# Two-layer decoder on one core: row-sum reciprocals spread over DRAM, the attention result copied by ScalarE and scaled in place by Pool

## The reference, cut to what matters

```python
x = _layernorm(x + _L0_attn_ref(...));  x = _layernorm(x + _L0_ffn_ref(...))
# _L1_attn_ref:
latent_kv = x @ w_kv_down
k, v = split(latent_kv @ w_kv_up);  q = x @ w_q           # 16 heads of 64
att = jnp.einsum('bqhd,bkhd->bhqk', q, k) * HEAD_SIZE ** -0.5
att = jax.nn.softmax(jnp.where(causal, att, -jnp.inf), axis=-1)
y = jnp.einsum('bhqk,bkhd->bqhd', att, v)
x = _layernorm(x + y.reshape(Bx, Tx, HD) @ w_out);  x = _layernorm(x + _L1_ffn_ref(...))
```

## Time and profile before

| | us |
|---|---|
| median of 3 runs (range) | 1919.13 (1919.01 to 1919.22) |
| the profiled execution | 1919.19 |
| its span, first to last instruction | 1917.1 |

### The profile page before, as it was taken

One profiled execution on the slowest core, in us unless ns is written; L12 is line 12 of the kernel. 1 busy time (PEld: TensorE's weight loads), 2 busy tenths in 40 slices (PEclk: granted clock), 3 DMA queues, 4 the chain that ended last, 5 costly groups with the idle time before them and its releaser, 6 DMA issues. The chain is left out here.

```text
span 1917.1 us, 42317 instructions
## 1 busy us (share of the span) xinstructions
PE 1703.5 (89%) x15702; PEld 1445.2 (75%) x15702; DVE 1362.2 (71%) x3230; ACT 1000.8 (52%) x2618; POOL 619.1 (32%) x975
## 2 busy tenths in 40 slices
PE   4599999899999999999988598999999999998895
PEld 3477778787877778877876365688888888888794
DVE  4688777877788777877775475566666666664777
ACT  2355555555555555565543354556566656652353
POOL 6455345543555335543451122000000000001653
PEclk9799999999999999999988799999999999999898
DMA  6212331323222332323320200990000000003232
GB/s 216 59 51 65 75 86 49 68 59 85 65 56 65 75 87 46 74 67 75 83 50 23 90 1 5 183 14 2 2 2 2 1 2 1 2 2 107 65 93 76
DMA packets 150338, 106.78 MB, mean 56 GB/s; under 512 B 34132, under 2 KB 138648, under 8 KB 149240
## 3 DMA queue, kind: packets, MB, share of 16 engines
q1 hardware_dynamic: 147640, 98.95, 23.7%
q0 software_dynamic: 2496, 5.13, 0.8%
HBM read 86.06 MB, written 17.99 MB: 54 GB/s over the span
## 5 line engine op out<-in xcount | busy, mean ns | idle before, releaser
L593 POOL TENSOR_TENSOR kfull<-kt,pair_rows 128x512 f32<-128x512 f32 x128 | 143.6, 1122 | 517.2 <-ACT kt L381 513.5
L361 PE MATMUL ps<-xT,taps 128*128 128x128 f32 x2048 | 276.8, 278 | 0.1
L853 ACT COPY wt<-ps 32x128 f32<-32x128 f32 x512 | 131.7, 257 | 263.9 <-PE ps L748 256.9
L361 PEld LDWEIGHTS ps<-xT,taps 128*128 128x128 f32 x2048 | 258.7, 196 | 7.6 <-issue 7.2
L1687 DVE TENSOR_REDUCE b_nmax<-ps 128x1 f32<-128x128 f32 (+7 forms) x256 | 180.6, 752 | 72.9 <-PE ps L1524 72.9
L896 DVE TENSOR_TENSOR prod<-ps,mt 128x128 f32<-128x128 f32 x512 | 147.4, 288 | 78.6 <-PE ps L759 62.7
L748 PE MATMUL ps<-ident,w 128*128 128x128 f32 x512 | 162.9, 318 | 34.6 <-ACT wt L853 18.5
L1664 POOL COPY b_spread<-b_inv 128x256 f32<-128x256 f32 x64 | 25.8, 402 | 513.2 <-DVE b_inv L1690 513.2
L899 DVE TENSOR_REDUCE w<-prod 128x32 f32<-128x128 f32 x512 | 146.5, 286 | 17.5
L748 PEld LDWEIGHTS ps<-ident,w 128*128 128x128 f32 x512 | 88.1, 172 | 84.9 <-DVE w L899 73.6
L1616 ACT ACTIVATE b_prob_long<-ps,b_nmax 128x1024 f32<-128x1024 f32 (+3 forms) x128 | 121.4, 953 | 55.7 <-DVE b_nmax L1687 55.7
(11 more groups left out here) (308 smaller groups left out, 3843.2 us busy)
## 6 DMA issues: line engine op xcount, KB each, us to landing
decay<-ends_dram SPq DMA_DIRECT2D x256, 128.0 KB, 5.5
gn<-near_dram SPq DMA_DIRECT2D x32, 384.0 KB, 6.9
slots_dram<-zero SPq DMA_DIRECT2D x1, 9216.0 KB, 59.3
rr<-rates_dram SPq DMA_DIRECT2D x32, 256.0 KB, 4.5
sq<-rstd_dram SPq DMA_DIRECT2D x16, 512.0 KB, 3.6
wtap<-in_taps SPq DMA_DIRECT2D x4, 1024.0 KB, 11.2
f_w<-in_f_w SPq DMA_DIRECT2D x2, 2048.0 KB, 10.4
s_xb<-slots_dram SPq DMA_DIRECT2D x46, 64.5 KB, 1.8
```

Of the source, the lines that this page charges most:

```text
L361: mm = pe.matmul(part, lhsT=taps[:, tap, t * P:(t + 1) * P], rhs=xT[:, :, columns(at_next) - LOOK + tap:columns(at_next) - LOOK + tap + TS ...
L593: nc.gpsimd.tensor_tensor(kfull[:, n % 4, :, :], kt[:, n % 2, :].unsqueeze(1).to_broadcast([P, G, P]), cst["pair_rows"][:, :].unsqueeze(2) ...
L853: nc.scalar.copy(wt[rows, b, :], ps[rows, 2, 0:P]).then_inc(wt_kept[b], 1)
```

## The change

The two transposes of the reciprocals, the Pool copy `spread` and DVE's `divide` are gone. In their place:

- SP stores `inv` of unit w (128 x 4, elements of 4 bytes) to a DRAM scratch `recips_dram`, waits for the store, and loads it back twice, each time into 64 partitions, as `recipT` (two buffers). Before the store of unit w it waits for `y_done` of unit w-2.
- ACT copies the undivided result from bank 7 to its place in `yT` (`keep_values`), where it copied the reciprocals before. `values(w)` now waits for this copy (`o_kept`).
- Pool multiplies that place in `yT` by `recipT`, in place.
- From unit 2 on, DVE's `reciprocal` also waits until the store of unit w-2 has landed, since it overwrites `inv`.
- The two DMAs into `slots_dram` are issued by ACT, after its copies of the first projections and ahead of the exponential of unit 0. SP waits for them at the end of the stage, as before.

```diff
-        spread = sb("spread", [P, 2, 4, AD])
-        recipT = sb("recipT", [P, 2 * P])
+        recipT = sb("recipT", [P, 2, 2 * P])
+        recips_dram = nc.dram_tensor("recips_dram", (2, 4, P), F32).ap()
...
                     if w:
-                        pe.wait_ge(y_done, w)
+                        pe.wait_ge(o_kept, w)
...
-                def turn_recips(w):
-                    pe.wait_ge(spread_done, w + 1)
-                    for long in range(2):
-                        mm = pe.transpose(ps[:, 7, (2 + long) * P:(3 + long) * P],
-                                          spread[:, w % 2, 2 * long:2 * long + 2, :].rearrange("p h c -> p (h c)"),
-                                          cst["ident"][:, :])
                     mm.then_inc(o_done, 1)
...
-                def keep_recips(w):
+                def keep_values(w):
                     act.wait_ge(o_done, w + 1)
-                    nc.scalar.copy(recipT[:, :], ps[:, 7, 2 * P:4 * P]).then_inc(recip_kept, 1)
+                    nc.scalar.copy(y_of(w), ps[:, 7, 0:2 * P].rearrange("p (i n t) -> p i n t", i=2,
+                                                                        n=P // TS)).then_inc(o_kept, 1)
...
+                slots = blank[2].rearrange("(k p) e -> p k e", p=P)
+                act.wait_ge(fill_made, 2)
+                nc.scalar.dma_start(slots[:, :, 0:C], blank[1][:, :].unsqueeze(1).to_broadcast(
+                    [P, slots.shape[1], C])).then_inc(filled, 16)
+                nc.scalar.dma_start(slots[:, :, C:ROW], blank[0][:, :].bitcast(F32).unsqueeze(2),
+                                    allow_slow_non_contiguous=True).then_inc(filled, 16)
                 for w in range(W):
                     for j in range(4):
                         exponent(w, j)
...
             @block.sync
+                for w in range(W):
+                    slot = recips_dram[w % 2]
+                    if w >= 2:
+                        sp.wait_ge(y_done, w - 1)
+                    sp.wait_ge(recip_done, w + 1)
+                    sp.dma_start(slot.rearrange("j q -> q j"), inv[:, w % 2, :],
+                                 allow_slow_non_contiguous=True).then_inc(recip_stored, 16)
+                    sp.wait_ge(recip_stored, 16 * (w + 1))
+                    for h in range(2):
+                        sp.dma_start(recipT[AD * h:AD * h + AD, w % 2, :].rearrange("c (l q) -> c l q", l=2),
+                                     slot[h:4:2, :].partition_broadcast(AD)).then_inc(recip_in[w % 2], 16)
...
             @block.gpsimd
-                    pool.wait_ge(recip_done, w + 1)
-                    nc.gpsimd.tensor_copy(spread[:, w % 2, :, :], inv[:, w % 2, :].unsqueeze(2).to_broadcast(
-                        [P, 4, AD])).then_inc(spread_done, 1)
+                    pool.wait_ge(recip_in[w % 2], 32 * (w // 2 + 1))
+                    pool.wait_ge(o_kept, w + 1)
+                    nc.gpsimd.tensor_tensor(y_of(w), y_of(w), recipT[:, w % 2, :].rearrange(
+                        "p (i n t) -> p i n t", i=2, n=P // TS), ALU.mult).then_inc(y_done, 1)
...
             @block.vector
                     dve.wait_ge(exp_done, 4 * w + 4)
+                    if w >= 2:
+                        dve.wait_ge(recip_stored, 16 * (w - 1))
                     nc.vector.reciprocal(inv[:, w % 2, :], total[:, w % 2, :]).then_inc(recip_done, 1)
-                    if w:
-                        divide(w - 1)
```

More of the change, by code:

```diff
@@ L1412, in softmax_attention, with y_of @@
             "lat_done", "lat_kept", "piece_done", "piece_kept_a", "piece_kept_v"))
-        s_done, max_done, exp_done, recip_done, spread_done, t_done, t_kept_a, t_kept_v, o_done, recip_kept, y_done = (
-            sem(n) for n in ("s_done", "max_done", "exp_done", "recip_done", "spread_done", "t_done", "t_kept_a",
-                             "t_kept_v", "o_done", "recip_kept", "y_done"))
+        s_done, max_done, exp_done, recip_done, recip_stored, t_done, t_kept_a, t_kept_v, o_done, o_kept, y_done = (
+            sem(n) for n in ("s_done", "max_done", "exp_done", "recip_done", "recip_stored", "t_done", "t_kept_a",
+                             "t_kept_v", "o_done", "o_kept", "y_done"))
+        recip_in = [sem("recip_in0"), sem("recip_in1")]
         every = [fill_made, filled, lat_done, lat_kept, piece_done, piece_kept_a, piece_kept_v, s_done, max_done, exp_done, recip_done,
-                 spread_done, t_done, t_kept_a, t_kept_v, o_done, recip_kept, y_done]
+                 recip_stored, t_done, t_kept_a, t_kept_v, o_done, o_kept, y_done] + recip_in
         units = [(hp, b, k) for hp in range(NP) for b in range(B) for k in range(TT // 2)]
         W, PW = len(units), B * TT // 2
+        def y_of(w):
+            hp, b, k = units[w]
+            return y_row[:, hp, b, k:TT - k:TT - 1 - 2 * k, :, :]
         def tile_of(w, long):
@@ L1555, in values @@
                                 cols = slice(AD * h, AD * h + AD)
-                                pe.matmul(ps[cols, 7, long * P:(long + 1) * P], lhsT=v[:, f, b * TT + j, cols],
-                                          rhs=probT[:, at_probT(w, long, h * n + j), :], start=(j == 0), stop=(j == n - 1),
-                                          skip_group_check=True)
-                def turn_recips(w):
-                    pe.wait_ge(spread_done, w + 1)
-                    for long in range(2):
-                        mm = pe.transpose(ps[:, 7, (2 + long) * P:(3 + long) * P],
-                                          spread[:, w % 2, 2 * long:2 * long + 2, :].rearrange("p h c -> p (h c)"),
-                                          cst["ident"][:, :])
+                                mm = pe.matmul(ps[cols, 7, long * P:(long + 1) * P], lhsT=v[:, f, b * TT + j, cols],
+                                          rhs=probT[:, at_probT(w, long, h * n + j), :], start=(j == 0),
+                                               stop=(j == n - 1), skip_group_check=True)
                     mm.then_inc(o_done, 1)
@@ L1590, in _ @@
                         values(w - 1)
-                        turn_recips(w - 1)
                     pieces = slot_pieces(w)
@@ L1600, in _ @@
                 values(W - 1)
-                turn_recips(W - 1)
             @block.scalar
@@ L1633, in _ @@
                     if w:
-                        keep_recips(w - 1)
+                        keep_values(w - 1)
                     hp = w // PW
@@ L1644, in _ @@
                                 "p (j t) -> p j t", t=P)).then_inc(t_kept_a, 1)
-                keep_recips(W - 1)
+                keep_values(W - 1)
             @block.sync
             def _(sp):
-                slots = blank[2].rearrange("(k p) e -> p k e", p=P)
-                sp.wait_ge(fill_made, 2)
-                sp.dma_start(slots[:, :, 0:C], blank[1][:, :].unsqueeze(1).to_broadcast(
-                    [P, slots.shape[1], C])).then_inc(filled, 16)
-                sp.dma_start(slots[:, :, C:ROW], blank[0][:, :].bitcast(F32).unsqueeze(2),
-                             allow_slow_non_contiguous=True).then_inc(filled, 16)
+                for w in range(W):
[9 more added lines that the diff above has]
+                                     slot[h:4:2, :].partition_broadcast(AD)).then_inc(recip_in[w % 2], 16)
+                for slot in range(2):
+                    sp.wait_ge(recip_in[slot], 32 * (W // 2))
                 sp.wait_ge(filled, 32)
@@ L1671, in keep_v @@
                         piece_kept_v, 1)
-                def divide(w):
-                    hp, b, k = units[w]
-                    dve.wait_ge(recip_kept, w + 1)
-                    view = "p (i n t) -> p i n t"
-                    nc.vector.tensor_tensor(y_row[:, hp, b, k:TT - k:TT - 1 - 2 * k, :, :],
-                                            ps[:, 7, 0:2 * P].rearrange(view, i=2, n=2),
-                                            recipT[:, :].rearrange(view, i=2, n=2), ALU.mult).then_inc(y_done, 1)
                 for n, piece in list(enumerate(FIRST))[8:]:
@@ L1702, in _ @@
                         keep_v(hp + 1, ps[:, 6, :], ROUND[n][1])
-                divide(W - 1)
         stage_end(nc, every)
```

## The result

| | us |
|---|---|
| before, median of 4 runs (range) | 1919.18 (1919.01 to 1921.45) |
| after, median of 4 runs (range) | 2209.25 (2205.91 to 2212.49) |
| ratio after / before, 95% interval | 1.151 (1.149 to 1.153) |
| profiled execution of after, its span | 2212.49, 2210.7 |

What follows compares the result with a forecast made beforehand. The prediction took PE to set the pace, DVE and ACT having room. Its terms 45.7 + 2.4 - 17.3 + 3.3 - 2.1 + 0.5 made +32.5 us on 1919.1: 1951.6 us, range 1938 to 1969.

Steps and rivals of the forecast that it cites:

- Part 1: Start of the stage: two DMAs issued by ACT ahead of its exponentials hold it and delay unit 0, +45.7 us.
- the two readings: The 50.80 us issue: spent on the second DMA's own 18432 pieces, or waiting for room behind the first DMA's 9216 KB.
- The first rival: ACT is not held by issuing the two DMAs, parts 1 and 2 vanish: 1903.5 us, chance 0.12.
- Part 2: PE after idling for ACT: its first products run at the lower granted clock, +2.4 us.
- Part 3: PE does two transposes less in each of 64 units, 0.27 us each by distance of starts: -17.3 us.
- Part 4: Without DVE's division, PE's masks behind k=1 units wait less for DVE's chunk copies: 16 x 0.13 = -2.1 us.
- What is given back: Part of PE's gain lost in 16 k=0 units (+2.7) and the last 8 units (+0.6): +3.3 us.
- Part 5: Reciprocals' round trip over SP and Pool: about 6 us per unit of 8, nothing in the steady loop, +0.5 at stage end.
- The rival of 0.02: The round trip over DRAM takes over 16 us, two units, and lengthens each unit: far above 1970, chance 0.02.
- The tail of +0.5: End of the stage: the last reciprocal's store, loads and product finish at about 1741.0 against 1740.54, +0.5 us.
- Second rival: First store on SP waits until ACT's indices have landed, delaying DVE's reciprocal of unit 2: +10.0, 1961.6 us, chance 0.17.
- Third rival: PE's freed 0.27 us turns into waiting for ACT in all units, part 3 falls away: 1965.6 us, chance 0.06.

Runs made afterwards that it cites:

- 16-byte version: Changed kernel, each reciprocal store written as 128 adjacent pieces of 16 bytes instead of 512 of 4, so wrong rows are scaled: 1954.83 us, +34.7.
- The version that gains: Changed kernel with 16-byte-row stores, correct loads of 511 floats, and zeros and indices issued by SP in 48 portions: 1927.31 us against 1936.97, ratio 0.9948.
- 512-byte version: Changed kernel, the 4-byte pieces of each store from unit 2 on written 512 bytes apart into another scratch: 1965.21 us, +45.1 against the kernel before.

## Why the prediction was wrong

The forecast was 1951.6 in 1938 to 1969, the measured time 2209.25.

**Part 1 was right.** +45.7 for ACT's hold; 47.9 in after, 42.2 in the kernel before with nothing else changed, 40.6 in the 16-byte version (the hold was 53.97, 48.42 and 47.61 us). Of the two readings, the one by which the 18432 pieces themselves cost the issuing engine 50 us has fallen: issued first, the same DMA takes 0.40 us. The other, of a queue that takes a bounded amount ahead, fits all runs. That is also how far the rule of the Trainium skill reaches that the prediction quoted (DMA: Bandwidth & Descriptors, "Issuing engines are not separate DMA queues"): the issue is short here, 0.40 us, where no large DMA is ahead of it, and 48 to 54 us where one is. The first rival fell.

**Part 2 was right**, a little large: +2.4 forecast, +1.6 in the kernel before and +2.0 in the 16-byte version.

**Part 3 was too large.** In the units with projections the gain is 0.17 us and not 0.27. The term took the distance of two starts. It did shrink by 0.28 us, but the projection that now follows the values directly needs 0.11 us more to reach the transposes. The lower bound, from the loading of two weights, was the better estimate. For the k=0 units the forecast 0.1 us is what came. In the last eight units, without projections, the prediction took 0.6 us off; there the gain was larger than elsewhere: their last 7 intervals make 49.2 us in the 16-byte version, 51.6 before, 0.33 us less each. Why, no run tells.

**Part 4 was wrong.** The masks behind a k=1 unit still take 0.52 us without DVE's division:

```profile
1466.98 0.52 PE L1507 MATMUL ps<-above_diag,ident 128*128 128x128 bf16 x4
```

The 0.13 us against the earlier trace rows weren't the division's doing; I had read them from one coincidence.

**What is given back** is better seen with parts 3 and 4 together: forecast -17.3 + 3.3 - 2.1 = -16.1 us. In the 16-byte version the 63 intervals make 506.3 us instead of 515.2, with 2.0 us of PE at its lower clock in them: -10.9. The version that gains, without that stall, also has -10.9.

**Part 5 is the step that failed**, twice. First in size: the store was put at 1.6 + 0.8 = 2.4 us, and took about 10 (7.9 to 11.9 behind the first two). The 0.8 us came from indices that were written 516 bytes apart, and such pieces do land in 1.8 us; the reciprocals' pieces touch. The earlier trace rows held no row with adjacent pieces of 4 bytes, and a bound from both sides should have said that the number of pieces was covered but their neighbourhood was not. Secondly in the threshold: "nobody in the loop waits for it closely", with 16 us as the point from which the round trip sets the pace. That was read from DVE's wait for a store two units old. But SP waits out each store before it issues the next, so one store is under way at a time, and the pace is set as soon as SP's own round (issue, landing, two issues of loads) is above the unit's 8.2 us. At 11.6 us it is, and the loop takes its period. The rival of 0.02 was the case that happened; with the right threshold, and a store whose price no row showed, it deserved much more. The tail of +0.5 was right for a quick store: the 16-byte version has +0.2 (last reciprocal +31.65, start of the next stage +31.86). In after it was +22.8. Pool's product, 0.7 us, took 0.72.

**Second rival**: its size came, +10.8 against +10.0 in the 512-byte version, but by luck, since not its way. It had the first store wait until the indices had landed, and unit 2 late by that. The first store lands before the indices do (1280.46 against 1301.99), only slowed, and it is the second slow store, behind it, that makes unit 3 late. In after both units are late:

```profile
1288.42 0.18 DVE L1695 RECIPROCAL b_inv<-b_total 128x4 f32<-128x4 f32 x1 [4.38 <-DMA recips_dram<-b_inv]
...
1310.79 0.18 DVE L1695 RECIPROCAL b_inv<-b_total 128x4 f32<-128x4 f32 x1 [12.68 <-DMA recips_dram<-b_inv]
```

The Trainium skill has the engines serve the queues in turn (the same page, "Queues, rings and completion order"), from which the prediction took that the delay would be small. That the store gets through at all beside the indices agrees with it. But small the delay is not: 16.1 us, and for the 128 pieces of 16 bytes 10.0 instead of 1.42. **Third rival**: fell in its form; the gain on PE came, smaller.

**The near hit of the 16-byte version was luck.** +34.7 against +32.5 looks like a sum that was right but for part 5. But the hold came out 5.1 us below its term (40.6 against 45.7), the gain on PE 5.2 us below its own (10.9 against 16.1), and the two errors cancel. Another slip had no effect: the sum of the upper bounds took 3.3 us for what is given back, whose bound was 4.9; with it the sum is 1967.6, still inside the range.

Of the 5 us behind the stage of the change in after, some 1.6 us go with PE's granted clock, which after the idle time at the end of the stage is 0.64 in the first 6 us of the next, against 1.00 before: the first result of that stage's first products reaches DVE 9.0 us after their start, instead of 7.4. The rest, and the 2.9 us in the 16-byte version, stay unexplained.

## What to carry to other kernels

For a round trip over DRAM inside a loop, add up the round of the engine that issues it, with the landing for which it waits, and hold that against the loop's period; the age of the buffer on the consumer's side is no slack if the issuer waits serially. Price a small store by its layout, not by its bytes or number of pieces: give each partition's values one run, or keep the pieces apart. And before a large DMA is moved to an engine that has other work, look whether a DMA stands ahead of it in the same queue; ahead of the others, or in portions, it cost half a microsecond to issue here.

## What the hardware showed that I had not expected

- 512 pieces of 4 bytes, 2 KB in all, take about 10 us when adjacent, 3.61 at 8 bytes apart, 2.43 at 16, 1.80 at 64, 1.78 at 512; 128 adjacent pieces of 16 bytes in 1.42.
- A store of 2 KB with adjacent pieces of 4 bytes takes 16 to 21 us while another queue writes 9 MB or the indices; with 128 pieces of 16 bytes it takes 10 and 12.
- The issue of one and the same DMA takes 0.40 us as the first of its queue and 48 to 54 us behind a DMA of 9 MB in that queue.
- Two transposes of 128x128 less, of 0.27 us by the distance of starts, shorten a unit with projections by 0.17 us.
